# Rotary query and key rows: copied out of PSUM by ScalarE, multiplied in place by VectorE one slot later, subtracted in the next; other pairs of tiles, moved stores, a split first norm

## The chip, the core and the metric

The kernel runs on one core of one Trainium2 chip. The metric is the device time in microseconds of one execution. Each core has TensorE (PE, matrix products into the PSUM banks), VectorE (DVE), ScalarE (ACT), GpSimd (POOL) and SyncE (SP, which here only issues DMAs). Engines run their own instruction streams in order and meet through semaphores.

## The reference, cut to what matters

The input x is (2, 512, 512). Two blocks of the form x = x + s * silu(g) follow each other. In the first, s is attention and g a gated feed-forward network, both of the same normed rows:

```python
qkv = hidden_states @ qkv_w + qkv_b              # 512 -> 3 * 512, 32 heads of 16
q = _rope(q, cos, sin); k = _rope(k, cos, sin)   # [x1*cos - x2*sin, x2*cos + x1*sin]
scores = jnp.einsum('bqhd,bkhd->bhqk', q, k) * scale
probs = jax.nn.softmax(scores + (1.0 - causal) * MASK_VAL, axis=-1)
ctx = jnp.einsum('bhqk,bkhd->bqhd', probs, v).reshape(b, s, e)
return ctx @ out_w + out_b
# the feed-forward part: silu(xt @ W_gate.T) * (xt @ W_up.T) @ W_down.T, 1376 wide
```

In the second block s is a four-layer recurrent network (a scan with complex decay, then a small MLP, per layer) and g a feed-forward network with ternary weights in an octonion arrangement. Everything is float32; products that need the precision are split into a rounded high part and a low part and take three passes.

## The kernel before, in words

The two sequences b = 0, 1 go through block 0 one after the other, then both through block 1 together. In block 0 the weights come in **units** of 128 x 512. Unit u is loaded by SP into `raw`, rounded to `w_hi` by ACT or POOL, and `w_lo = raw - w_hi` is made by POOL. Units 0 and 1 are the first 128 columns of Q and K, units 2 to 5 are V, and `Q_UNIT`, `K_UNIT` and `FFN_UNIT` give the places of the rest. Each Q, K or feed-forward unit becomes one **job**: twelve matmuls of 128x512 (L942 to L944) into one of two banks `proj_ps`.

The attention part is a table of **slots**. In slot s (0 to 47) PE multiplies the scores of one pair of heads (L972, group of tiles x = s % 3), VectorE adds the mask and takes the row maxima (L1486, `row_maxima`), and PE may only start the scores of slot s + 1 when these are done (`part_ready`). Five slots behind (`LAG`) PE makes the transposed scores (L981, `scores_T`) and ACT their exponentials (L1344), which PE waits for before the next transposed scores (`probs_ready`). The rest of PE's slot is two "triples" of the running job (`fill`), the product with V, and turns. One sequence has 65 slots; in the last 17 come the down projection and the turns of the next norm. Every engine runs the same table: `for s in range(SLOTS)` with `units_after(s)` (the jobs that ended in slot s - 1), `rest_in_slot`, `written_in`, `read_in` and `raw_in_slot` saying what it does in slot s.

A Q or K job is followed by the rotation: three VectorE instructions that read the bank in PSUM, add the bias and multiply by the cosine or sine (`rope_first`, L1538 to L1542), in the slot in which the job is known to be done, behind that slot's row maxima. One slot later VectorE adds the two halves (`rope_second`, L1553), ACT rounds the sum (`rope_hi`, L1278), POOL makes the low part (`rope_lo`, L770), and SP writes all of it to DRAM (`write_rows`, L660 and L662). `read_rows` (L675) brings it back as the stacks `q_st` and `k_st` of one group of four heads; group g is needed by the scores of slot 6g.

SP's queue is in order. At slot 1 of the first sequence it also holds six stores of the ternary weights (L708), in front of the read of group 1. The first norm: VectorE takes statistics of four tiles (L1499), then aggregates (L1502), POOL makes the inverse deviation of all four at once (L833, L835), VectorE scales (L1508), PE turns 16 blocks (L1018), ACT and VectorE split them (L1262, L1475).

## Time and profile before

| | |
|---|---|
| median of 3 runs | 640.64 us (639.93, 640.64, 642.9) |
| the profiled execution's own time | 639.16 us |
| its span (first to last instruction) | 637.3 us |
| outside the span | 1.9 us |
| PE busy | 603.5 us, 95% |
| VectorE busy | 383.8 us, 60% |
| GpSimd busy | 376.9 us, 59% |
| ScalarE busy | 276.7 us, 43% |

Busy shares say which engine has no time to spare on the whole; here it is PE. What a change can save is then the time in which PE stood, or ran at a lower clock. The ends of matmuls are modelled in the profile, so a short stall shows as less idle time than it cost: the start of one slot's scores to the start of the next is the safer measure.

### The profile page before, as it was taken

Reading aid. Unit: us, or ns where it says so; the run is one execution under the profiler, and the core shown is the slowest. Engines: PE = TensorE matmul, PEld = TensorE weight load, DVE = VectorE, ACT = ScalarE, POOL = GpSimd, SP = SyncE. Lnnn points to the kernel's source line nnn. Section 1 sums busy time; section 2 is a strip of 40 time slices with the busy share of each in tenths; the row PEclk is TensorE's granted clock in tenths of the full one; section 3 lists DMA queues with packets and bytes.
Section 4 is the critical chain, followed back from the end, with each engine's and each line's share of the span. In section 5 each row is a group of like instructions: output and inputs, shape, how many; then the busy total and the mean of one; then the engine's idle time right before and its main releaser. Section 6 shows DMA issues by size and latency. Waiting matters only on the chain.

```text
span 637.3 us, 9817 instructions
## 1 busy us (share of the span) xinstructions
PE 603.5 (95%) x3348; PEld 417.2 (65%) x3348; DVE 383.8 (60%) x920; ACT 276.7 (43%) x440; POOL 376.9 (59%) x596
## 2 busy tenths in 40 slices
PE   2998998999999999888999999999999999999996
PEld 2865565666657888655656665677878676767664
DVE  4957867666524587696686664264986261525257
ACT  3524554655553533054555556444222344332432
POOL 4875756655434577767566544345888676641264
PEclk9998999999999999999999999999999999999999
DMA  9768764744441335658568644643440000000002
GB/s 291 220 227 282 214 200 129 230 118 103 96 129 54 95 92 165 194 179 262 139 165 261 187 113 123 259 161 115 144 164 1 0 1 1 1 1 0 1 30 103
DMA packets 60369, 83.63 MB, mean 131 GB/s; under 512 B 17936, under 2 KB 26768, under 8 KB 60320
## 3 DMA queue, kind: packets, MB, share of 16 engines
q1 hardware_dynamic: 57392, 73.70, 39.2%
q10 hardware_dynamic: 2928, 9.31, 4.0%
q8 instruction: 27, 0.44, 0.3%
q14 instruction: 22, 0.18, 0.1%
HBM read 65.17 MB, written 26.99 MB: 145 GB/s over the span
## 4 chain that ended last, share of the span: by engine, by line
PE 73%; DVE 9%; DMA 6%; POOL 4%; issue 3%; SPq 2%; ACT 2%; ACTq 0%; POOLq 0%; DVEq 0%
PE proj_ps L942 8%; PE ctx_ps L1097 6%; PE proj_ps L943 6%; PE proj_ps L944 6%; PE score_ps L972 5%; PE proj_ps L1145 3%; PE proj_ps L1146 3%; PE scoreT_ps L981 3%; DMA k_st<-rows 3%; PE score_ps L942 2%; PE score_ps L944 2%; PE score_ps L943 2%; PE ctx_ps L1145 2%; PE scoreT_ps L1145 2%; PE scoreT_ps L1146 2%
## 5 line engine op out<-in xcount | busy, mean ns | idle before, releaser
L761 POOL TENSOR_TENSOR w_lo<-raw,w_hi 128x512 fp32r<-128x512 f32 x98 | 133.1, 1363 | 68.1 <-ACT w_hi L1300 61.7
L1486 DVE CUSTOM_DVE_ANT_0 score_ps<-score_ps,causal 128x512 f32<-128x512 f32 (+3 forms) x256 | 119.9, 516 | 59.5 <-PE score_ps L972 59.0
L1344 ACT ACTIVATE probs_T<-scoreT_ps 128x1024 f32<-128x1024 f32 (+1 forms) x96 | 84.9, 884 | 79.1 <-PE scoreT_ps L981 78.6
L942 PE MATMUL proj_ps<-xn_hi,w_hi 128*128 128x512 f32 x224 | 99.9, 446 | 0.3 <-POOL w_lo L761 0.3
L943 PE MATMUL proj_ps<-xn_hi,w_lo 128*128 128x512 f32 x224 | 88.3, 394 | 0.0
L944 PE MATMUL proj_ps<-xn_lo,w_hi 128*128 128x512 f32 x224 | 88.2, 394 | 0.0
L759 POOL TENSOR_SCALAR w_hi<-raw 128x512 fp32r<-128x512 f32 x50 | 31.2, 625 | 49.7 <-PE proj_ps L944 47.2
L942 PEld LDWEIGHTS proj_ps<-xn_hi,w_hi 128*128 128x128 f32 x224 | 42.0, 187 | 24.6 <-issue 9.8
L972 PE MATMUL score_ps<-k_st,q_st 50*128 50x512 f32 (+3 forms) x256 | 44.7, 386 | 13.2 <-DVE row_max L1486 7.8
L972 PEld LDWEIGHTS score_ps<-k_st,q_st 50*128 50x128 f32 x256 | 21.8, 186 | 53.8 <-issue 26.8
L795 POOL TENSOR_SCALAR_AFFINE_SELECT probs_T<-probs_T 128x256 f32<-128x256 f32 x128 | 49.6, 410 | 9.8 <-ACT probs_T L1344 9.8
L917 POOL TENSOR_TENSOR hsL<-hidden_T,hsH 128x256 fp32r<-128x256 f32 x44 | 38.0, 882 | 26.6 <-ACT hsH L1427 26.1
L944 PEld LDWEIGHTS proj_ps<-xn_lo,w_hi 128*128 128x128 f32 x224 | 42.2, 188 | 9.8
L1097 PE MATMUL ctx_ps<-probs_T,V 128*32 128x128 f32 (+3 forms) x512 | 47.7, 445 | 0.0
L943 PEld LDWEIGHTS proj_ps<-xn_hi,w_lo 128*128 128x128 f32 x224 | 42.5, 190 | 5.0
L1269 ACT ACTIVATE q_st<-one_turn_ps 2x512 fp32r<-2x512 f32 x64 | 37.5, 585 | 18.8 <-PE one_turn_ps L958 18.5
L1616 DVE TENSOR_TENSOR hsl<-hidden_T,hsh 128x512 fp32r<-128x512 f32 x22 | 16.2, 735 | 40.9 <-ACT hsh L1367 40.9
L981 PE MATMUL scoreT_ps<-q_st,k_st 50*128 50x512 f32 (+3 forms) x256 | 37.5, 329 | 0.7 <-ACT probs_T L1344 0.7
L1300 ACT ACTIVATE w_hi<-raw 128x512 fp32r<-128x512 f32 x48 | 30.0, 625 | 18.1 <-PE one_turn_ps L944 6.9
L1486 DVE DVE_READ_ACCUMULATOR2_ANT row_max<- 128x1 f32 x256 | 35.5, 139 | 0.3
L925 POOL TENSOR_TENSOR inv_std<-var_eps,half 128x8 f32<-128x8 f32 x9 | 14.8, 1646 | 34.6 <-DVE var_eps L1760 34.6
L1278 ACT ACTIVATE rows_hi<-turned_rows 128x512 fp32r<-128x512 f32 x16 | 10.1, 632 | 49.8 <-DVE turned_rows L1553 41.6
(306 smaller groups left out, 1317.2 us busy)
## 6 DMA issues: line engine op xcount, KB each, us to landing
raw<-w SPq DMA_DIRECT2D x98, 256.0 KB, 2.8
rows<-rows_hi SPq DMA_DIRECT2D x32, 256.0 KB, 3.7
arranged<-tern SPq DMA_DIRECT2D x96, 85.0 KB
q_st<-rows SPq DMA_DIRECT2D x32, 200.0 KB
k_st<-rows SPq DMA_DIRECT2D x32, 200.0 KB
rows<-rows_lo SPq DMA_DIRECT2D x16, 256.0 KB, 4.5
gate_w<-arranged ACTq DMA_DIRECT2D x4, 704.0 KB, 7.1
up_w<-arranged ACTq DMA_DIRECT2D x4, 704.0 KB, 8.4
```

Of the source, the lines that this page charges most:

```text
L761: nc.gpsimd.tensor_tensor(w_lo[n % SPLIT][:, :], raw[n % RAW][:, :], F32(w_hi[n % SPLIT][:, :]), ALU.subtract).then_inc(unit_ready, 1)
L795: m = nc.gpsimd.affine_select(out=halves[:, :, c:c + P], in_=halves[:, :, c:c + P], pattern=[[0, 2], [1, P]], compare_op=ALU.is_ge, fill=0 ...
L917: nc.gpsimd.tensor_tensor(hsL[d % HS][:, :], hidden1_T[:, f, 256 * pr:256 * pr + 256], F32(hsH[d % HS][:, :]), sub).then_inc(hs1_ready, 1)
L942: nc.tensor.matmul(acc, lh, rh, start=first, stop=False)
L943: nc.tensor.matmul(acc, ll, rh, start=False, stop=False)
L944: return nc.tensor.matmul(acc, lh, rl, start=False, stop=last)
L972: m = nc.tensor.matmul(score_ps[:, hh, c:c + (qt + 1) * P], q[:, qt * P:(qt + 1) * P], k[:, 0:(qt + 1) * P], start=part == 0, stop=True, s ...
L981: m = nc.tensor.matmul(scoreT_ps[:, hh, c:c + S - kt * P], k[:, kt * P:(kt + 1) * P], q[:, kt * P:], start=part == 0, stop=True, skip_grou ...
L1097: m = nc.tensor.matmul(ctx_ps[32 * h:32 * h + 32, kt * P:S], V[:, kt, (4 * g + h) * 32:(4 * g + h + 1) * 32], probs_T[(gp + h // 2) % 4][: ...
L1145: nc.tensor.matmul(hid1_ps[u % 4], lhs, xh[:, kc, :], start=kc == 0, stop=False)
L1344: nc.scalar.activation(probs_T[gp % 4][:, c:c + 2 * w].rearrange("p (h c) -> p h c", h=2), scoreT_ps[:, :, 0:w], ACT.Exp, scale=0.25).then ...
L1486: m = nc.vector.tensor_tensor_reduce(out=block, in0=block, in1=causal[:, S - w:], scale=1.0, scalar=-3e38, op0=ALU.add, op1=ALU.max, accum ...
```

## The change

The diff, with small parts left out:

```diff
@@ -52,8 +52,8 @@
...
 UNITS = U_OUT + KC
-Q_UNIT, K_UNIT, V_UNIT = (0, 9, 12, 18), (1, 10, 13, 19), 2
-FFN_UNIT = [6, 7, 8, 11, 14, 15, 16, 17] + list(range(20, 34))
+Q_UNIT, K_UNIT, V_UNIT = (0, 8, 12, 18), (1, 9, 13, 19), 2
+FFN_UNIT = [6, 7, 10, 11, 14, 15, 16, 17] + list(range(20, 34))
 IN_FRONT = 3 * KC
...
 TRIPLES = (U_DOWN - FILL) * KC
@@ -62,6 +62,10 @@
 FFN_OF = {u: w for w, u in enumerate(FFN_UNIT)}
+COPIED = [u for u in sorted(QK_OF) if u >= FILL]
 def job(u):
...
@@ -103,15 +107,15 @@
 def rest_in_slot(s):
-    return [u for u in sorted(QK_OF) if u >= FILL and unit_slot(u) + 3 == s]
+    return [u for u in sorted(QK_OF) if u >= FILL and unit_slot(u) + 4 == s]
 def written_in(s):
-    return [u for u in sorted(QK_OF) if u >= FILL and unit_slot(u) + 4 == s]
+    return [u for u in sorted(QK_OF) if u >= FILL and unit_slot(u) + 5 == s]
 def read_in(s):
-    return next((g for g in range(1, GROUPS) if (1 if g == 1 else max(6 * g - 6, unit_slot(K_UNIT[g // 2]) + 6)) == s), None)
+    return next((g for g in range(1, GROUPS) if (1 if g == 1 else max(6 * g - 6, unit_slot(K_UNIT[g // 2]) + 7)) == s), None)
 def down_in(s):
@@ -191,6 +195,7 @@
 HI_BY_ACT = FILL + 3
...
 RAW, SPLIT = 4, 5
+WARM = 10
 COPIES = (50, 49)
...
@@ -631,7 +637,13 @@
...
-        return proj_free, JOBS * b + job(u) + 1
+        return job_released(b, job(u))
+    def job_released(b, n):
+        copied_jobs = [job(u) for u in COPIED]
+        if n in copied_jobs:
+            return rope_copied, len(COPIED) * b + copied_jobs.index(n) + 1
+        return proj_free, (JOBS - len(COPIED)) * b + sum(k not in copied_jobs for k in range(n + 1))
...
@@ -639,7 +651,7 @@
         def _(sp):
...
                 sp.dma_start(X[:, t, :], x_dram[0, t]).then_inc(x_in[t], 16)
-                if t == 0:
+                if t == NT - 1:
                     sp.dma_start(ident[:, :], A["ident"]).then_inc(ident_in, 16)
...
@@ -701,17 +713,16 @@
                         write_rows(b, K_UNIT[0])
...
                 for s in range(SCORE_SLOTS + 1):
-                    if b == 0 and s == 1:
-                        for w in range(3):
-                            sp.wait_ge(wp_ready, w + 1)
-                            for x, src in enumerate((tern_pos[w], tern_neg[w])):
-                                sp.dma_start(tern_d[w][x].rearrange("(p n) -> p n", p=P), F32(src[:, :])).then_inc(tern_stored, 16)
                     for u in written_in(s):
...
                         read_rows(b, read_in(s))
-                    for u in raw_in_slot(s):
+                    for x, u in enumerate(raw_in_slot(s)):
                         load(b, u)
+                        if b == 0 and s == 0 and 1 <= x <= 3:
+                            sp.wait_ge(wp_ready, x)
+                            for half, src in enumerate((tern_pos[x - 1], tern_neg[x - 1])):
+                                sp.dma_start(tern_d[x - 1][half].rearrange("(p n) -> p n", p=P), F32(src[:, :])).then_inc(tern_stored, 16)
                     if b == 0 and s == 3:
...
                     for x in range(copies_in(b, s)):
@@ -831,11 +842,16 @@
...
                 nc.gpsimd.tensor_scalar(var_eps0[:, :], mean_var[:, :, 1], EPS, 1.0, ALU.add, ALU.mult).then_inc(eps_added, 1)
-                pool.wait_ge(eps_added, k + 1)
+                pool.wait_ge(eps_added, k + 2)
                 nc.gpsimd.tensor_tensor(rstd[:, :], var_eps0[:, :], half[:, 0:NT], ALU.pow).then_inc(rstd_ready, 1)
             pool.wait_ge(ones_set, 2)
-            norm_rstd(0)
+            for x in range(2):
+                pair = slice(2 * x, 2 * x + 2)
+                pool.wait_ge(mv_ready, 2 * x + 2)
+                nc.gpsimd.tensor_scalar(var_eps0[:, pair], mean_var[:, pair, 1], EPS, 1.0, ALU.add, ALU.mult).then_inc(eps_added, 1)
+                pool.wait_ge(eps_added, x + 1)
+                nc.gpsimd.tensor_tensor(rstd[:, pair], var_eps0[:, pair], half[:, 0:2], ALU.pow).then_inc(rstd_ready, 1)
             for b in range(B):
...
                 for u in range(FILL):
@@ -982,8 +998,6 @@
                                              start=part == 0, stop=True, skip_group_check=part > 0)
...
-            pe.wait_ge(ident_in, 16)
             def norm_turn(k, chunks=range(KC)):
                 pe.wait_ge(xn_ready, NT * (k + 1))
@@ -999,7 +1013,7 @@
                 if kc == 0:
...
                     if job(u) >= 2:
-                        pe.wait_ge(proj_free, JOBS * b + job(u) - 1)
+                        pe.wait_ge(*job_released(b, job(u) - 2))
                     elif b:
...
                 wh, wl = unit(b, u)
@@ -1012,6 +1026,10 @@
                 for k in triples_in(s):
...
+            pe.wait_ge(ones_set, 2)
+            for n in range(WARM):
+                nc.tensor.matmul(proj_ps[1][:, 0:P], V[:, 0, 0:P], V[:, 0, 0:P], start=True, stop=True)
+            pe.wait_ge(ident_in, 16)
             for t in range(NT):
...
                 for kc in range(KC):
...
@@ -1276,6 +1294,16 @@
                 if r >= 2:
...
                 nc.scalar.activation(rows_hi[t][:, :], turned_rows[t][:, :], ACT.Copy).then_inc(rows_hi_ready, 1)
+            def rope_copy(b, u):
+                (t, c), r = QK_OF[u], rope_job(b, u)
+                ps, bias = job_bank(u), qk_bias[:, 4 * t + c:4 * t + c + 1]
+                act.wait_ge(proj_done, JOBS * b + job(u) + 1)
+                act.wait_ge(turned_ready, r - 1)
+                nc.scalar.activation(by_cos[t][:, :], ps[:, :], ACT.Identity, bias=bias)
+                nc.scalar.activation(by_sin[t][0:64, :], ps[64:128, :], ACT.Identity, bias=bias[64:128])
+                nc.scalar.activation(by_sin[t][64:128, :], ps[0:64, :], ACT.Identity, bias=bias[0:64]).then_inc(rope_copied, 1)
...
@@ -1352,7 +1380,9 @@
                     for u in units_after(s):
...
                             ffn_tanh(b, u)
-                    for u in units_after(s - 1):
+                        else:
+                            rope_copy(b, u)
+                    for u in units_after(s - 2):
                         if u in QK_OF:
...
                     if max_in(s) is not None:
@@ -1381,7 +1411,7 @@
                         act.wait_ge(arranged, 16 * len(ARRANGE))
...
                         load_rows(W_UP, up_w1, tu_in, range(2, KC))
-                    if b == B - 1 and s == LAST_DOWN - 1:
+                    if b == B - 1 and s == LAST_DOWN - 2:
...
                                          (bout[:, :], A["bout"].partition_broadcast(P))):
@@ -1494,16 +1524,28 @@
                 if k:
...
                 for t in range(NT):
-                    if k == 0:
-                        dve.wait_ge(x_in[t], 16)
                     nc.vector.bn_stats(stat[:, t, :], NORM[k][0][:, t, :]).then_inc(stats, 1)
...
+            def first_stats(t):
+                dve.wait_ge(x_in[t], 16)
+                nc.vector.bn_stats(stat[:, t, :], X[:, t, :]).then_inc(stats, 1)
+                dve.wait_ge(stats, t + 1)
+                nc.vector.bn_aggr(mean_var[:, t, :], stat[:, t, :]).then_inc(mv_ready, 1)
+            def first_rows(t):
+                dve.wait_ge(mv_ready, t + 1)
+                dve.wait_ge(rstd_ready, t // 2 + 1)
+                nc.vector.tensor_scalar(xn_first[:, t, :], X[:, t, :], mean_var[:, t, 0:1], rstd[:, t:t + 1],
+                                        ALU.subtract, ALU.mult).then_inc(xn_ready, 1)
             def norm_rows(k):
                 dve.wait_ge(mv_ready, NT * (k + 1))
-                dve.wait_ge(rstd_ready, k + 1)
+                dve.wait_ge(rstd_ready, k + 2)
                 for t in range(NT):
...
                                             ALU.subtract, ALU.mult).then_inc(xn_ready, 1)
@@ -1542,6 +1584,13 @@
                 nc.vector.scalar_tensor_tensor(out=by_sin[t][64:128, :], in0=ps[0:64, :], scalar=bias[0:64], in1=rope_sin[0:64, :],
...
+            def rope_times(b, u):
+                (t, c), r = QK_OF[u], rope_job(b, u)
+                dve.wait_ge(*released(b, u))
+                nc.vector.tensor_tensor(by_cos[t][:, :], by_cos[t][:, :], rope_cos[:, :], ALU.mult).then_inc(cos_ready, 1)
+                nc.vector.tensor_tensor(by_sin[t][:, :], by_sin[t][:, :], rope_sin[:, :], ALU.mult).then_inc(sin_half, 1)
             def rope_second(b, u):
                 (t, c), r = QK_OF[u], rope_job(b, u)
@@ -1550,7 +1599,9 @@
                 dve.wait_ge(*released(b, u))
...
                     dve.wait_ge(rows_lo_ready, r - 1)
-                nc.vector.tensor_tensor(turned_rows[t][:, :], by_cos[t][:, :], by_sin[t][:, :], ALU.add).then_inc(turned_ready, 1)
+                nc.vector.tensor_tensor(turned_rows[t][:, :], by_cos[t][:, :], by_sin[t][:, :], ALU.subtract if u in COPIED else ALU.add)\
+                    .then_inc(turned_ready, 1)
...
@@ -1558,8 +1609,10 @@
                     rope_first(b, u)
...
-            norm_stats(0)
-            norm_rows(0)
+            for t in range(NT):
+                first_stats(t)
+            for t in range(NT):
+                first_rows(t)
             norm_lo(0)
...
             nc.vector.tensor_copy(ident_r[:, :], ident[:, :]).then_inc(ident_rounded, 1)
@@ -1583,7 +1636,8 @@
                         nc.vector.scalar_tensor_tensor(out=tern_neg[w][:, :], in0=tern_w[w][:, :], scalar=theta[:, 1, w:w + 1], in1=tern_over[w][:, :],
...
                 for u in units_after(0):
-                    ffn_out(b, u)
+                    if u in FFN_OF:
+                        ffn_out(b, u)
                 for s in range(SLOTS):
...
                         row_maxima(b, s)
@@ -1602,14 +1656,15 @@
                                                 c3[:, :, 0:D].rearrange("p (t h) d -> p t h d", t=NT),
...
                                                 ALU.mult).then_inc(turn_done(n), 1)
+                    for u in units_after(s - 2):
+                        if u in QK_OF:
+                            rope_second(b, u)
                     for u in units_after(s - 1):
                         if u in QK_OF:
-                            rope_second(b, u)
+                            rope_times(b, u)
                     for u in units_after(s) if s else ():
...
                             ffn_out(b, u)
-                        else:
-                            rope_first(b, u)
                     if parted_in(s) is not None:
...
```

In words: in the slot in which a Q or K job (other than the first two) is known to be done, ACT copies the bank out, with the bias, in three ACTIVATEs (`rope_copy`); they free the bank, so PE now waits on `rope_copied` for it. VectorE multiplies both copies in place one slot later (`rope_times`, two instructions of 128x512), and subtracts them one slot after that. Six jobs per sequence go this way, twelve in all. One pair of tiles of Q and K moves to units 8 and 9 (from 9 and 10), so that its rows are written and read back a slot or more earlier; the later pairs are written a slot later. The ternary stores stand between the weight loads of slot 0. The first norm is split into two halves, ten matmuls on a tile of ones (`WARM`) precede the first turns, `ident` is loaded behind X, and four DMA issues on ACT's queue stand one slot earlier near the end of block 0.

VectorE's order around the job of unit 12, which ends in slot 7 of a sequence (`proj_ps` holds it; the rows are those of slots 8 to 10, the maxima rows that repeat left out). Before:

```order
L1486 ISA score_ps,row_max<-score_ps,causal 128x256
L1486 ISA row_max 128x1
L1538 SCALAR_TENSOR_TENSOR by_cos_79<-proj_ps,qk_bias,rope_cos 128x512
L1540 SCALAR_TENSOR_TENSOR by_sin_81<-proj_ps,qk_bias,rope_sin 64x512
L1542 SCALAR_TENSOR_TENSOR by_sin_81<-proj_ps,qk_bias,rope_sin 64x512
L1486 ISA score_ps,row_max<-score_ps,causal 128x512
L1486 ISA row_max 128x1
...
L1553 TENSOR_TENSOR turned_rows_83<-by_cos_79,by_sin_81 128x512
L1486 ISA score_ps,row_max<-score_ps,causal 128x384
```

Now:

```order
L1516 ISA score_ps,row_max<-score_ps,causal 128x256
L1516 ISA row_max 128x1
...
L1516 ISA score_ps,row_max<-score_ps,causal 128x512
L1516 ISA row_max 128x1
L1591 TENSOR_TENSOR by_cos_79<-by_cos_79,rope_cos 128x512
L1592 TENSOR_TENSOR by_sin_81<-by_sin_81,rope_sin 128x512
L1516 ISA score_ps,row_max<-score_ps,causal 128x384
L1516 ISA row_max 128x1
...
L1603 TENSOR_TENSOR turned_rows_83<-by_cos_79,by_sin_81 128x512
```

Three instructions between the maxima of slots 8 and 9 are gone; two stand between those of slots 9 and 10, and the subtraction is behind the maxima of slot 10.

ScalarE's order in the same slots (`probs_T` are the exponentials, `q_st` the rows of maxima). Before:

```order
L1344 ACTIVATE probs_T_95<-scoreT_ps 128x1024 x2
L1278 ACTIVATE rows_hi_85<-turned_rows_83 128x512
L1269 ACTIVATE q_st_90<-one_turn_ps 2x512 x2
L1344 ACTIVATE probs_T_95<-scoreT_ps 128x512
L1344 ACTIVATE probs_T_96<-scoreT_ps 128x1024 x2
```

Now:

```order
L1372 ACTIVATE probs_T_95<-scoreT_ps 128x1024
L1304 ACTIVATE by_cos_79<-proj_ps,qk_bias 128x512
L1305 ACTIVATE by_sin_81<-proj_ps,qk_bias 64x512
L1306 ACTIVATE by_sin_81<-proj_ps,qk_bias 64x512
L1372 ACTIVATE probs_T_95<-scoreT_ps 128x1024
L1287 ACTIVATE q_st_90<-one_turn_ps 2x512 x2
L1372 ACTIVATE probs_T_95<-scoreT_ps 128x512
L1296 ACTIVATE rows_hi_85<-turned_rows_83 128x512
L1372 ACTIVATE probs_T_96<-scoreT_ps 128x1024
```

Three copies have come between the exponentials of slots 8 and 9, and the rounding of the rows has moved from in front of the maxima rows to behind the next exponential.

SyncE's order at slots 0 and 1 of the first sequence. Before:

```order
L652 DMA raw_101<-w 128x512
L708 DMA tern<-tern_pos_151 128x680
L708 DMA tern<-tern_neg_154 128x680
L708 DMA tern<-tern_pos_152 128x680
L708 DMA tern<-tern_neg_155 128x680
L708 DMA tern<-tern_pos_153 128x680
L708 DMA tern<-tern_neg_156 128x680
L675 DMA q_st_90<-rows 50x2x512 x2
```

Now:

```order
L664 DMA raw_101<-w 128x512
L725 DMA tern<-tern_pos_151 128x680
L725 DMA tern<-tern_neg_154 128x680
L664 DMA raw_102<-w 128x512
L725 DMA tern<-tern_pos_152 128x680
L725 DMA tern<-tern_neg_155 128x680
L664 DMA raw_103<-w 128x512
L725 DMA tern<-tern_pos_153 128x680
L725 DMA tern<-tern_neg_156 128x680
L664 DMA raw_100<-w 128x512
L664 DMA raw_101<-w 128x512
L687 DMA q_st_90<-rows 50x2x512 x2
```

The read of group 1 (`q_st_90`) has no store right in front of it any more.

## Rows read from the trace of the kernel before

**Rows 1.** The page, busy time of TensorE.

```profile
PE 603.5 (95%) x3348; PEld 417.2 (65%) x3348; DVE 383.8 (60%) x920; ACT 276.7 (43%) x440; POOL 376.9 (59%) x596
```

**Rows 2.** Timeline, PE, score matmuls: start, us, instruction, count [idle before <-releaser].

```profile
269.84 0.44 PE L972 MATMUL score_ps<-k_st,q_st 50*128 50x384 f32 x2 [0.66 <-DVE row_max L1486]
272.07 0.39 PE L972 MATMUL score_ps<-k_st,q_st 50*128 50x256 f32 x2
275.18 0.50 PE L972 MATMUL score_ps<-k_st,q_st 50*128 50x512 f32 x2 [0.90 <-DVE row_max L1486]
277.67 0.50 PE L972 MATMUL score_ps<-k_st,q_st 50*128 50x384 f32 x4
...
281.34 0.50 PE L972 MATMUL score_ps<-k_st,q_st 50*128 50x512 f32 x2
284.81 0.45 PE L972 MATMUL score_ps<-k_st,q_st 50*128 50x384 f32 x2 [0.77 <-DVE row_max L1486]
287.05 0.38 PE L972 MATMUL score_ps<-k_st,q_st 50*128 50x256 f32 x2
291.37 0.50 PE L972 MATMUL score_ps<-k_st,q_st 50*128 50x512 f32 x2 [1.48 <-DMA k_st<-rows]
...
329.48 0.44 PE L972 MATMUL score_ps<-k_st,q_st 50*128 50x384 f32 x2 [0.92 <-DVE row_max L1486]
```

**Rows 3.** Timeline, VectorE, slots 8 and 9 of the second sequence.

```profile
281.07 0.75 DVE L1538 SCALAR_TENSOR_TENSOR by_cos<-proj_ps,qk_bias,rope_cos 128x512 f32<-128x512 f32 x1
```

**Rows 4.** Line queries: duration ns min/median/max of one.

```profile
L1553 DVE TENSOR_TENSOR turned_rows<-by_cos,by_sin x16: 685/694/1076, 20.5 to 329.3; 128x512 f32<-128x512 f32 x16
L761 POOL TENSOR_TENSOR w_lo<-raw,w_hi x98: 1265/1293/1920, 11.8 to 440.3; 128x512 fp32r<-128x512 f32 x98
```

**Rows 5.** Groups of ACT by form: count | busy us, mean ns | idle before.

```profile
L1393 ACT ACTIVATE ctx_hi<-proj_ps,v_bias 128x512 fp32r<-128x512 f32 x4 | 2.7, 683 | 0.0
```

**Rows 6.** The view of waits, PE, whole span: us in total, times, longest.

```profile
PE scoreT_ps L981 <- ACT probs_T L1344: 0.7, 2, 0.4
```

**Rows 7.** Timeline, ScalarE, slots 9 and 10 of the second sequence.

```profile
282.25 1.03 ACT L1344 ACTIVATE probs_T<-scoreT_ps 128x1024 f32<-128x1024 f32 x1 [0.60 <-PE scoreT_ps L981]
285.34 0.63 ACT L1278 ACTIVATE rows_hi<-turned_rows 128x512 fp32r<-128x512 f32 x1 [2.06 <-DVE turned_rows L1553]
```

**Rows 8.** Timeline, TensorE, first sequence, in slot 11.

```profile
70.58 0.50 PE L981 MATMUL scoreT_ps<-q_st,k_st 50*128 50x512 f32 x2 [0.38 <-ACT probs_T L1344]
```

**Rows 9.** Timeline, first sequence, start of slot 1, on PE.

```profile
42.73 0.44 PE L972 MATMUL score_ps<-k_st,q_st 50*128 50x384 f32 x2 [0.76 <-DVE row_max L1486]
```

**Rows 10.** Timeline, SP's queue and PE, first sequence, slots 1 to 6.

```profile
46.77 1.20 SPq L708 DMA_DIRECT2D tern<-tern_neg  x1
48.02 1.83 SPq L675 DMA_DIRECT2D q_st<-rows  x2
...
56.51 0.50 PE L972 MATMUL score_ps<-k_st,q_st 50*128 50x512 f32 x2 [2.19 <-DMA k_st<-rows]
```

**Rows 11.** Windows: us, busy PE PEld DVE ACT POOL (x), PEclk, DMA share, GB/s.

```profile
57.90:61.30 3.40, 3.40 (x16) 2.50 (x15) 1.73 (x6) 1.74 (x4) 2.36 (x5) 0.51 0.82 289
```

**Rows 12.** Timeline, the head: VectorE, TensorE, ScalarE.

```profile
9.79 1.92 DVE L1508 TENSOR_SCALAR xn_first<-X,mean_var,rstd 128x512 f32<-128x512 f32 x4 [1.59 <-POOL rstd L835]
...
10.48 0.45 PE L1018 MATMUL one_turn_ps<-ident,xn_first 128*128 128x128 f32 x1 [10.48 <-DVE xn_first L1508]
...
13.07 0.42 PE L1018 MATMUL one_turn_ps<-ident,xn_first 128*128 128x128 f32 x1
...
14.90 0.50 PE L942 MATMUL score_ps<-xn_hi,w_hi 128*128 128x512 f32 x1 [0.98 <-DVE xn_lo L1475]
```

**Rows 13.** Timeline, ScalarE, the first sum of absolute weights.

```profile
16.74 0.76 ACT L1289 ACTIVATE tern_over<-tern_w 128x680 f32<-128x680 f32 x1
```

**Rows 14.** The page of DMA issues, SP: out<-in, count, KB, median us to landing.

```profile
tern_w<-tern_w SPq DMA_DIRECT2D x3, 340.0 KB, 6.0
```

**Rows 15.** Timeline, TensorE, end of block 0's second sequence.

```profile
439.98 0.66 PE L938 MATMUL one_turn_ps<-ident,ctx_rows 128*128 128x128 f32 x4 [1.14 <-DVE ctx_lo L1626]
```

5 lines of the change are left out of this document (3 added, 2 removed).

## The prediction

> **What bounds the kernel now.** I read the page's busy times first: TensorE is busy for 603.5 us of a span of 637.3 [rows 1], so only what lets it stand, or slows it, can be won. Then the timeline of TensorE's score matmuls, by the start of each slot [rows 2]. A slot that has score group x = 0 and the turns of the maxima lasts 2.49 us where nothing holds it (275.18 to 277.67), and 3.47 where a rotation lies behind its maxima (281.34 to 284.81): 0.98 lost. The reader should see the pattern behind it: idle times of 0.66, 0.90, 0.77 and 0.92 us, all ended by VectorE's row maxima, stand at the places where VectorE was still at the rotation. The fifth such place in this sequence is before slot 23. By the view of waits TensorE waited for the exponentials only twice, 0.7 us together [rows 6]: ScalarE, 43% busy, has been out of its way.
>
> The profiled execution took 639.16 us, 1.48 less than the median of 640.64. I sum against 639.16 and shift the result to the median.
>
> **Rotation, each sequence.** Before, three VectorE instructions of 0.75 us each [rows 3], 2.25 in all, follow a slot's maxima, and TensorE's next slot waits for maxima queued behind them. Five of six jobs cost: slots 3, 5, 9, 22 and 24. Slots 5 and 24 have 0.90 and 0.92 idle, slot 9 loses 0.98 by its starts and slot 3 has 0.66 idle of which some 0.5 is net of a later slot (3.00 against 2.49 long); slot 22 is like it with 0.7. I take 0.5 + 1.0 + 1.0 + 0.7 + 1.0 = 4.2 a sequence, 8.4 in all; the idle entries alone, 0.66 + 0.90 + 0.77 + 0.7 + 0.92 = 3.95, would make 7.9. The job of unit 13 costs nothing visible now.
>
> After, VectorE has two multiplications, 1.4 us by the subtraction's 0.69 [rows 4], one slot after the copies, and the subtraction, 0.69, one slot later. A lone 0.69 behind the maxima costs nothing today (slots 4, 10). 1.4 is 0.85 less than 2.25, so where 2.25 lost 1.0 it loses 0.15, except where the multiplications fall on a slot whose maxima already set its length. With 2.23-us slots of x = 1 of that kind (269.84 to 272.07 [rows 2]) I estimate 0.3 at slot 2, 0.1 at slot 4 and 0.4 at slot 10: 0.8 a sequence, 1.6 in all. Bounds: 0, if all of it lies beside other work, and 1.4 x 12 = 16.8 if none does.
>
> ScalarE takes on three copies. The nearest row is its reading of a PSUM bank with a bias, 0.68 for 128x512 [rows 5]; reading SBUF it is 0.63, and an exponential twice as wide takes 1.03, so 0.52 a half [rows 7]. Three copies are 1.6 to 2.05 us, I take 1.9, twelve times 23 us of ScalarE's idle time. They free the bank, which before was freed by VectorE at 2.25 after its maxima; the job after next wants it at least a slot and a half later, so this costs nothing. The rounding of the rows moves two slots on: where it stood ahead of the exponentials it held ScalarE for 2.06 us, waiting for VectorE's sum [rows 7]. That wait goes, as the sum is by then long done. The copy itself waits for its job's last matmul, which ended in the slot before.
>
> Net of this part: 8.4 - 1.6 = **6.8 us**.
>
> **Pair 8, 9 instead of 9, 10.** Stack g2 is needed at slot 12. In the second sequence slot 11 (287.05 to 291.37, 4.32 long) ends in a wait for its DMA, 1.48 idle [rows 2]. Slot 5 of the same group lasts 3.11 with a rotation's 0.98, so 2.13 is clean and slot 11 loses 2.19. The units come a slot earlier for Q and for K, and the read is issued at slot 8 instead of 9, a slot being worth 2.2 to 2.5 us: it just covers the 2.19. In the first sequence TensorE waits there for the exponentials, 0.38 idle [rows 8], as ScalarE has been held by the same rounding; I count 0.65 by the slot's length. Sum **2.8 us**, bounds 0.6 (the transfer is as late as before) and 2.8.
>
> **Ternary stores.** At slot 1 of the first sequence the read of group 1 is issued at 48.02, right behind the last store [rows 10], while slot 1 begins at 42.73 [rows 9]: 5.3 us, of which some 0.8 are SP's own issues. Slot 6 then stands 2.19 us for this transfer [rows 10]. Of the 2.19, 0.98 would be the rotation's, as in the second sequence, and is counted above; 1.3 is this wait's (the slot is 2.28 longer than clean). With the read 4.5 us earlier it goes. The stores stand between weight loads one slot earlier; they delay the loads of three units, which have a slot or more of slack. 
>
> **Slot 0, first sequence.** The product of unit 8 stood behind the first maxima there; slot 1 starts with 0.76 idle [rows 9]. Unit 8 is now a K or Q tile and VectorE has nothing at slot 0: **0.8 us**, bounds 0 and 0.8. ScalarE's three copies stand there instead, ahead of no exponential.
>
> **Head.** The inverse deviations of all four tiles come 1.59 us after the statistics; the four scalings take 1.92 from 9.79, the 16 turns start at 10.48 and are 0.216 apart (12 of them to 13.07), and the first projection starts at 14.90 [rows 12]. Split by halves, the first two tiles are scaled while the second half's deviation is made; the last is ready about 10.6 instead of 11.7, and only its four turns remain. With ten matmuls ahead, the turns should be as fast as at the other end of the kernel, four in 0.66 [rows 15]. The last turn ends at about 11.3 and the first projection, 1.38 behind ScalarE's first rounding now (13.52), starts at about 12.4: 2.5 us earlier. But the products with V behind the two projections need the sums of absolute weights. The first now starts at 16.74 and takes 0.76 [rows 13]; their DMA lands some 6.0 us after its issue [rows 14], about 16.2, so the third sum is done at 16.2 + 3 x 0.78 = 18.6, and V starts at 18.7 instead of 20.6. I take **1.9 us**; bounds 0.5 (the weights' load moves on too) and 2.65 (nothing else is late).
>
> The Trainium skill ("TensorE: Matmul & The Clock Gate", Part 1: The HAM clock gate) says that an idle TensorE goes to the lower level and that earlier matmuls lift it. By that rule the ten matmuls pay and the stop ahead of slot 6 costs twice, and rows 11 agree for the stop (after 2.19 us of standing [rows 10]); for the head only the 0.216 between turns speaks for the lower level. Without the rule's part the head would be 0.5 us later at the turns, and V's start would not move.
>
> **Tail.** At the end of block 0's second sequence TensorE stands 1.14 us for `ctx_lo` [rows 15], behind ScalarE's DMA issues. One slot earlier they are out of the way of ScalarE's context rounding, but stand in front of other work: **0.15 us**, bounds -0.3 and 1.14.
>
> **Port contention.** The multiplications read two SBUF tiles; `rope_first` read one and PSUM. The subtraction, of the same kind, has a median of 694 ns but takes 1076 at worst, and GpSimd's `w_lo` 1293 and 1920 [rows 4]. I take **-0.8 us**, bounds 0 and -5.
>
> The Trainium skill ("SBUF — State Buffer", SBUF: two separate sides) says that a VectorE operation with two SBUF inputs and a GpSimd operation that reads SBUF hold a shared port pair exclusively, each for the whole instruction. The longest of rows 4 agree, 0.38 and 0.63 above the median, their medians do not; by that rule in full, each of 24 multiplications could wait 1.29. This speaks against the change, and is rival 2 below, priced from rows.
>
> **Sum.** 6.8 + 2.8 + 2.8 + 0.8 + 1.9 + 0.15 - 0.8 = 14.45, say 14.5. 639.16 - 14.5 = 624.7; to the median + 1.48: **626.1**, forecast 626.0.
>
> **Rivals.**
> 1. The row transfers stay late. They are written one slot later for every pair but the first and read only then; if the DMA, not the issue, is the limit, the 2.19 of slot 11 and the 1.3 of slot 6 stay in good part. For it: 1.48 idle on the transfer alone; against: the clear 5.3 us of queue. It gives back 3.3: 629.4.
> 2. Port contention at the worst of each kind: 24 multiplications at 1.076 instead of 0.69 are 9.2 us, of which about half shows behind maxima: 4.2 more than taken, 630.3. Against it is the median.
> 3. ScalarE takes VectorE's place in part. In the slot of the copies it has 2 x 1.03 + 1.9 = 3.96 us of work in a slot of 2.23 to 2.49. If TensorE waits 0.3 us of it per job, 12 x 0.3 = 3.6: 629.7. For it: rows 8; against: rows 6.
> 4. The other side: the same, without any slack behind. The exponentials of the copies' slot come 3.96 - 2.23 = 1.73 us late and TensorE waits for all of it at 12 jobs, 20.8 us, in place of the 1.6 taken above as new cost: 14.45 + 1.6 - 20.8 = -4.75, so 639.16 + 4.75 + 1.48 = 645.4. It decides where the wait exceeds some 1.3 us a job (16 / 12). Against it: the next slots have 2.06 + 0.63 of work at most, and the transposed scores run five slots behind.
>
> **How the numbers follow.** Chances: the forecast 0.58, rival 1 0.17, rival 2 0.10, rival 3 0.10, rival 4 0.05. The forecast's own range, from the bounds of the head, the tail and the slots, is 623 to 629. Rivals 1 to 3 end at 629.4 to 630.3, two together at 633; 622.5 to 632.5 leaves out rival 4, most of such pairs and a tail of the forecast. 0.5% of 640.6 is 3.2 us, about what can be told from no change: faster means below 637.4, slower above 643.8. All cases but rival 4 and a mixture halfway to it are faster: 0.94, 0.03 and 0.03.
>
> **What would show it.** Right: score slots 3, 5, 9, 22 and 24 without idle time ended by the maxima; at 57 to 61 us no granted clock of 0.5; slot 11 of the second sequence about 2.1 long; the read of group 1 issued within a microsecond of slot 1; V's first product about 18.7; ScalarE's waits for `turned_rows` gone; TensorE's waits for exponentials under 2 us in all. Wrong: idle entries of the score matmuls ended by `k_st` (rival 1), multiplications of `rope_times` with a median near 1.0 us (rival 2), transposed scores that wait for `probs_T` in the slots after a copy (rivals 3 and 4), or a V stage that starts where it does now, at 20.6. If the sum is right but the time is not, the loss should lie in the 17 slots after the scores or in block 1, which this sum leaves alone.

## The result, and the profile after

The changed kernel takes 634.1 us (median of 6 runs, 631.3 to 636.1); the kernel before 641.05 (median of 6, 637.7 to 642.9). The ratio is 0.9891, with a 95% interval of 0.9865 to 0.9916: 7 us faster, where 14.5 were forecast and 626.0 was the time. The direction was right; the time lies 1.6 us above the range's upper end (632.5).

The profiled execution took 631.3 us, 7.9 below the 639.16 of before. The page's busy times, to be read against [rows 1]:

```profile
PE 605.8 (96%) x3368; PEld 419.6 (67%) x3368; DVE 382.3 (61%) x908; ACT 300.0 (48%) x476; POOL 384.5 (61%) x598
```

ScalarE has taken on 23.3 us, as priced (23). VectorE has given up only 1.5 us, though 36 instructions of 0.75 us became 24 that were priced at 0.69: 10.4 us should have gone. That is the first sign of what failed.

TensorE's score matmuls in the second sequence, slots 4 to 13 (columns as in [rows 2]), with one row that stands inside slot 12:

```profile
264.44 0.50 PE L988 MATMUL score_ps<-k_st,q_st 50*128 50x384 f32 x4
268.20 0.39 PE L988 MATMUL score_ps<-k_st,q_st 50*128 50x256 f32 x2 [1.68 <-DVE row_max L1516]
270.34 0.50 PE L988 MATMUL score_ps<-k_st,q_st 50*128 50x512 f32 x2
272.83 0.50 PE L988 MATMUL score_ps<-k_st,q_st 50*128 50x384 f32 x4
275.06 0.39 PE L988 MATMUL score_ps<-k_st,q_st 50*128 50x256 f32 x2
276.50 0.50 PE L988 MATMUL score_ps<-k_st,q_st 50*128 50x512 f32 x2
279.09 0.50 PE L988 MATMUL score_ps<-k_st,q_st 50*128 50x384 f32 x4
...
281.78 0.39 PE L988 MATMUL score_ps<-k_st,q_st 50*128 50x256 f32 x2
283.92 0.51 PE L988 MATMUL score_ps<-k_st,q_st 50*128 50x512 f32 x2
286.17 0.47 PE L958 MATMUL proj_ps<-xn_hi,w_hi 128*128 128x512 f32 x1 [0.62 <-ACT by_sin L1306]
288.26 0.51 PE L988 MATMUL score_ps<-k_st,q_st 50*128 50x384 f32 x4
```

The stalls of [rows 2] are gone: slot 5 lasts 2.14, slot 9 2.59, and slot 11 2.14 with no DMA behind it. But slot 4 lasts 3.76 instead of 2.23, and slot 12 4.34 instead of 3.49. The idle column shows only 0.62 of slot 12's 0.85; the starts are the measure.

Lengths of the slots that moved, by the starts of their score matmuls in the profiled executions (us; first / second sequence; clean is what the slot takes where nothing holds it; for slot 3 the prediction's 2.49 stands, though it takes 2.26):

| slot | before | clean | after |
|---|---|---|---|
| 0 | 2.85 / 2.02 | 2.02 | 2.03 / 2.01 |
| 2 | 1.88 / 1.90 | 1.88 | 2.50 / 2.45 |
| 3 | 3.02 / 3.00 | 2.49 | 2.26 / 2.27 |
| 4 | 2.23 / 2.23 | 2.23 | 3.77 / 3.77 |
| 5, 6, 7 | 10.58 / 7.84 | 6.86 | 6.86 / 6.86 |
| 9 | 3.47 / 3.47 | 2.49 | 2.57 / 2.59 |
| 10 | 2.24 / 2.24 | 2.24 | 2.66 / 2.69 |
| 11 | 2.78 / 4.32 | 2.13 | 2.14 / 2.14 |
| 12 | 3.48 / 3.49 | 3.48 | 4.34 / 4.34 |
| 22, 23, 24 | 10.00 / 9.98 | 8.30 | 8.84 / 8.86 |
| 26 | 2.02 / 2.02 | 2.02 | 2.18 / 2.18 |

So the rotation's stalls fell from 8.4 us not to 1.6 but to 8.0: 0.6 at slot 2, 1.5 at slot 4, 0.1 at 9, 0.4 at 10, 0.9 at 12, 0.5 at 23 and 0.2 at 26, less 0.2 at slot 3, 4.0 a sequence. (With 2.26 as the clean length of slot 3 both sums would be 0.5 larger, and their difference the same.) Between the last scores of the first sequence and the first of the second lie 91.6 us instead of 90.8.

VectorE across slots 3 and 4, and GpSimd beside it:

```profile
264.19 1.40 DVE L1591 TENSOR_TENSOR by_cos<-by_cos,rope_cos 128x512 f32<-128x512 f32 x1
265.51 1.09 DVE L1592 TENSOR_TENSOR by_sin<-by_sin,rope_sin 128x512 f32<-128x512 f32 x1
...
268.01 0.68 DVE L1603 TENSOR_TENSOR turned_rows<-by_cos,by_sin 128x512 f32<-128x512 f32 x1
```

```profile
263.75 1.29 POOL L781 TENSOR_TENSOR rows_lo<-turned_rows,rows_hi 128x512 fp32r<-128x512 f32 x1 [0.39 <-ACT rows_hi L1296]
265.00 1.07 POOL L770 TENSOR_SCALAR w_hi<-raw 128x512 fp32r<-128x512 f32 x1
266.15 1.57 POOL L772 TENSOR_TENSOR w_lo<-raw,w_hi 128x512 fp32r<-128x512 f32 x1
```

The first multiplication begins while `rows_lo` runs (to 265.04) and ends 0.55 later; the second ends 0.53 behind the end of `w_hi` (266.07). Each ends about half a microsecond after GpSimd's instruction ends, as if it had waited for that. GpSimd's instructions behind them are longer too: `w_hi` takes 1.07 instead of 0.62, `w_lo` 1.57 instead of 1.29.

Over the whole execution, from the queries of the two lines (min/median/max in ns):

```profile
L1591 DVE TENSOR_TENSOR by_cos<-by_cos,rope_cos x12: 686/985/1401, 42.2 to 320.8; 128x512 f32<-128x512 f32 x12
L1592 DVE TENSOR_TENSOR by_sin<-by_sin,rope_sin x12: 683/1096/1765, 43.0 to 322.2; 128x512 f32<-128x512 f32 x12
```

The same query for the instruction of the kernel before that reads PSUM and one SBUF tile:

```profile
L1538 DVE SCALAR_TENSOR_TENSOR by_cos<-proj_ps,qk_bias,rope_cos x12: 741/747/748, 46.1 to 325.7; 128x512 f32<-128x512 f32 x12
```

It never varied, though `w_lo` or `rows_lo` ran beside most of them. ScalarE ahead of slot 12:

```profile
282.51 0.63 ACT L1296 ACTIVATE rows_hi<-turned_rows 128x512 fp32r<-128x512 f32 x1 [0.99 <-DVE turned_rows L1603]
283.05 1.01 ACT L1372 ACTIVATE probs_T<-scoreT_ps 128x1024 f32<-128x1024 f32 x1
283.96 0.68 ACT L1304 ACTIVATE by_cos<-proj_ps,qk_bias 128x512 f32<-128x512 f32 x1
284.65 0.69 ACT L1305 ACTIVATE by_sin<-proj_ps,qk_bias 64x512 f32<-64x512 f32 x1
285.35 0.68 ACT L1306 ACTIVATE by_sin<-proj_ps,qk_bias 64x512 f32<-64x512 f32 x1
286.05 1.03 ACT L1372 ACTIVATE probs_T<-scoreT_ps 128x1024 f32<-128x1024 f32 x1
```

Its rounding of the rows still waits for VectorE's sum (24.6 us in all, against 41.6 before), and the three copies end at 286.03, where TensorE wanted the bank at 285.5.

In slot 10 it is not the bank. There the exponentials start right behind the copies, and TensorE waits for them before its transposed scores:

```profile
278.09 0.68 ACT L1306 ACTIVATE by_sin<-proj_ps,qk_bias 64x512 f32<-64x512 f32 x1
278.80 1.02 ACT L1372 ACTIVATE probs_T<-scoreT_ps 128x1024 f32<-128x1024 f32 x1
```

```profile
279.88 0.39 PE L997 MATMUL scoreT_ps<-q_st,k_st 50*128 50x256 f32 x2 [0.29 <-ACT probs_T L1372]
315.78 0.50 PE L997 MATMUL scoreT_ps<-q_st,k_st 50*128 50x512 f32 x2 [0.28 <-ACT probs_T L1372]
```

The second of these rows is in slot 23. With the two of the first sequence that makes four such waits, 1.1 us by the idle column. By the starts, the transposed scores of slot 10 come 0.79 us behind its scores, against 0.34 in slot 7, which has the same work: these 0.45 us are all that slot 10 lost.

The head and the first read of rows, TensorE, ScalarE and SP's queue:

```profile
9.54 0.27 PE L1036 MATMUL proj_ps<-ident,xn_first 128*128 128x128 f32 x1
9.65 0.27 PE L1036 MATMUL scoreT_ps<-ident,xn_first 128*128 128x128 f32 x1
...
12.04 0.50 PE L958 MATMUL score_ps<-xn_hi,w_hi 128*128 128x512 f32 x1 [1.08 <-DVE xn_lo L1505]
18.55 0.35 PE L1049 MATMUL proj_ps<-abs_sums,V 128*128 128x3 f32 x2 [0.74 <-ACT tern_over L1317]
```

```profile
16.03 0.77 ACT L1317 ACTIVATE tern_over<-tern_w 128x680 f32<-128x680 f32 x1 [2.07 <-DMA tern_w<-tern_w]
```

```profile
42.95 0.76 SPq L687 DMA_DIRECT2D q_st<-rows  x2
```

The turns are 0.11 apart, not 0.216 [rows 12]; the first projection starts 2.9 us earlier, and V's stage waits for the sums, as forecast. The read is issued at 42.95 instead of 48.02 [rows 10]. At the end of block 0's second sequence TensorE waits longer than in [rows 15]:

```profile
432.75 0.66 PE L954 MATMUL one_turn_ps<-ident,ctx_rows 128*128 128x128 f32 x4 [1.47 <-DVE ctx_lo L1681]
```

### The profile page after: what moved, and what is told of

Its sections match the earlier page's. It is cut to its first block, busy times and chain, and to the rows that moved or that the text cites. A ratio compares the mean times of both kernels' runs of the same rounds, so it can differ in the third digit from the quotient of the medians.

```text
span 629.4 us, 9886 instructions
## 1 busy us (share of the span) xinstructions
PE 605.8 (96%) x3368; PEld 419.6 (67%) x3368; DVE 382.3 (61%) x908; ACT 300.0 (48%) x476; POOL 384.5 (61%) x598
## 4 chain that ended last, share of the span: by engine, by line
PE 50%; ACT 2%; DVE 2%; POOL 2%; issue 1%; ACTq 0%; POOLq 0%; DVEq 0%
PE proj_ps L958 4%; PE proj_ps L1163 3%; PE proj_ps L1164 3%; PE ctx_ps L1115 3%; PE proj_ps L959 3%; PE proj_ps L960 3%; PE score_ps L988 2%; PE ctx_ps L1163 2%; PE scoreT_ps L1163 2%; PE ctx_ps L1164 2%; PE scoreT_ps L1164 2%; PE scoreT_ps L997 2%; PE one_turn_ps L1242 1%; POOL hsL L933 1%; PE proj_ps L1170 1%; PE score_ps L1262 1%
## 5 line engine op out<-in xcount | busy, mean ns | idle before, releaser
L770 POOL TENSOR_SCALAR w_hi<-raw 128x512 fp32r<-128x512 f32 x50 | 34.1, 681 | 41.7 <-PE proj_ps L960 37.3
L806 POOL TENSOR_SCALAR_AFFINE_SELECT probs_T<-probs_T 128x256 f32<-128x256 f32 x128 | 52.3, 428 | 11.4 <-ACT probs_T L1372 11.4
L1397 ACT ACTIVATE hsh<-hidden_T 128x512 fp32r<-128x512 f32 x22 | 13.9, 631 | 39.2 <-PE score_ps L960 39.2
```

What stands on the lines that cost most here:

```text
L806: m = nc.gpsimd.affine_select(out=halves[:, :, c:c + P], in_=halves[:, :, c:c + P], pattern=[[0, 2], [1, P]], compare_op=ALU.is_ge, fill=0 ...
```

## The experiments

Two theories stood after this reading. **P**: multiplications with two SBUF inputs wait for GpSimd's instructions that read SBUF. **S**: ScalarE gets to the copies late and is long at them, so TensorE waits for the bank that they free, or for the exponentials behind them. The rival to both was the prediction's own step, that the copies pay 6.8 us. Ratios are against the kernel before, with 95% intervals; the changed kernel's is 0.9891.

**e1, the rotation given back to VectorE.**

```diff
-COPIED = [u for u in sorted(QK_OF) if u >= FILL]
+COPIED = []
...
-                    for u in units_after(s - 1):
+                    for u in units_after(s):
                         if u in QK_OF:
-                            rope_times(b, u)
...
+                            rope_first(b, u)
...
```

With it the sum, the rounding and the writing and reading of the rows go back one slot.

> The changed kernel with the rotation given back to VectorE (three instructions from PSUM behind the maxima of the slot in which the job is done, the sum one slot later, rows written and read at the old distances); head, moved stores, pair 8 and 9 and the tail stay as changed. Theory P (the multiplications in place lose to GpSimd's port what they save, and TensorE waits for ScalarE's copies): the twelve rotations then cost as much either way, and this kernel takes the changed kernel's time within 1.5 us, about 633 to 636; its slots 3, 5, 9, 22, 24 lose 0.5 to 1.0 us each again, and slots 4 and 12 lose nothing. The prediction's term (6.8 us for the copies): it is 6 to 7 us slower than the changed kernel, 640 to 642.

637.8 us, 0.9955 (0.9932 to 0.9978): 4 us slower than the changed kernel by the ratios, between the two expectations. Its stalls were 1.5 at slot 1 (the job of unit 8 now ends ahead of slot 0), 1.0 at 9, 0.65 at 11 (TensorE waits for the exponentials there, as in [rows 8]), 0.7 at 22 and 1.0 at 24, with the rest at slots 2 to 5. So the copies are worth 4 us beside the new pair, though only 0.4 against the stalls of the old placing: the new pair puts a rotation in front of a slot that VectorE fills, and without the copies that costs. Part of what this trace lost is the clock's: in the second sequence the granted clock fell to 0.68 and 0.75 (264 to 270) behind the stop of slot 1, and again to 0.68 (440 to 444) behind a wait of 2.04 us for `ctx_lo` at the end of block 0.

**e2, the low part of the weights filled with zeros.**

```diff
-                nc.gpsimd.tensor_tensor(w_lo[n % SPLIT][:, :], raw[n % RAW][:, :], F32(w_hi[n % SPLIT][:, :]),
-                                        ALU.subtract).then_inc(unit_ready, 1)
+                nc.gpsimd.memset(F32(w_lo[n % SPLIT][:, :]), 0.0).then_inc(unit_ready, 1)
```

> The changed kernel in which GpSimd fills w_lo with zeros instead of subtracting (the low part of the weights is left out of the products): the instruction reads nothing of SBUF. Theory P: multiplications that lay beside w_lo fall from 0.9 to 1.8 us towards 0.69, their mean under 0.85; those beside w_hi or rows_lo, which still read, stay long; slots 2, 4 and 23 lose 1 us less together in each sequence, and the time falls by 2 to 4 us. Rival (VectorE's long instructions are long for another reason, such as the copies' writing into the same rows): the mean stays near 1.0 us and the time within 1 us.

628.3 us, 0.9818 (0.9783 to 0.9853). Unit 13's multiplications fell from 1.12 and 1.76 us to 0.79 and 0.68, but those beside `w_hi` stayed at 1.10, and those beside `rows_lo` at 1.27 to 1.40. (The 1.12 and the 0.79 both lay beside `w_hi` and ended 0.54 behind it; that one only began later. The 1.76 was `w_lo`'s.) The mean of all 24 went from 1.06 to 0.92 us, where under 0.85 was expected. Slot 4 fell by 0.3, slot 2 by 0.1, slots 12 and 23 not at all. 2.3 us of the gain came from the stretch between the sequences, which GpSimd's shorter work shortens: the time was no clean test, the durations were.

**e5, GpSimd fills `w_hi` and `rows_lo` as well.** The edit of `w_lo` is that of e2.

```diff
-                    nc.gpsimd.tensor_scalar(w_hi[n % SPLIT][:, :], raw[n % RAW][:, :], 1.0, 0.0, ALU.mult, ALU.add).then_inc(hi_done, 1)
+                    nc.gpsimd.memset(F32(w_hi[n % SPLIT][:, :]), 0.0).then_inc(hi_done, 1)
...
-                nc.gpsimd.tensor_tensor(rows_lo[t][:, :], turned_rows[t][:, :], F32(rows_hi[t][:, :]), ALU.subtract).then_inc(rows_lo_ready, 1)
+                nc.gpsimd.memset(F32(rows_lo[t][:, :]), 0.0).then_inc(rows_lo_ready, 1)
```

> The changed kernel in which GpSimd fills w_lo, its share of w_hi, and rows_lo with zeros (those parts of the weights and of the rotated rows are left out of the products): of GpSimd's long instructions none reads SBUF. Theory P: every multiplication and subtraction of VectorE that lay beside them falls to 0.68 to 0.70 us, and slot 4 loses 0.3 to 0.6 us against 2.24 instead of 1.54, slot 2 0.3 instead of 0.55; slots 10, 12 and 23 stay as long as they are, since they wait for ScalarE. Rival (slot 4 is long by VectorE's own work): slot 4 stays above 3.4 us.

625.1 us, 0.9765 (0.9715 to 0.9815). The two lines of the multiplications, and slot 4 of the second sequence:

```profile
L1590 DVE TENSOR_TENSOR by_cos<-by_cos,rope_cos x12: 686/690/693, 42.4 to 314.9; 128x512 f32<-128x512 f32 x12
L1591 DVE TENSOR_TENSOR by_sin<-by_sin,rope_sin x12: 682/684/894, 43.0 to 315.5; 128x512 f32<-128x512 f32 x12
```

```profile
260.09 0.50 PE L987 MATMUL score_ps<-k_st,q_st 50*128 50x384 f32 x4
262.51 0.39 PE L987 MATMUL score_ps<-k_st,q_st 50*128 50x256 f32 x2 [0.33 <-DVE row_max L1515]
```

Slot 4 lasts 2.42 and slot 2 1.93; slots 10 and 23 stay, 12 falls only to 4.08. P is shown: it held 0.5 us at slot 2 and 1.35 at slot 4 of each sequence, and the 0.2 of slot 26 (2.01 now). It is the same two instructions, in the same place; only what GpSimd did beside them differs. The two long ones left (0.894 each) lay beside the causal mask, an in-place instruction of GpSimd. As with e2 the time is no clean test: 2.3 us of it came from the stretch between the sequences, and slot 5 of the first sequence rose to 2.80, because TensorE, earlier now, waits 0.60 us for the stack of group 1.

**e3, two copies instead of three.**

```diff
-                nc.scalar.activation(by_sin[t][0:64, :], ps[64:128, :], ACT.Identity, bias=bias[64:128])
-                nc.scalar.activation(by_sin[t][64:128, :], ps[0:64, :], ACT.Identity, bias=bias[0:64]).then_inc(rope_copied, 1)
+                nc.scalar.activation(by_sin[t][:, :], ps[:, :], ACT.Identity, bias=bias).then_inc(rope_copied, 1)
```

> The changed kernel with two copies of 128x512 on ScalarE instead of three (by_sin is copied in one instruction, so its halves are not exchanged and the rotation is wrong by that). Theory S (TensorE waits for its bank because ScalarE gets to the copies late and they take 3 x 0.69): slot 12 loses 0.2 instead of 0.85 us in each sequence, slots 2 and 4 stay as they are, time 1.0 to 1.8 us below the changed kernel. If only the ports matter, slot 12 stays at 4.34 us and the time within 0.5 us.

628.6 us, 0.9828 (0.9793 to 0.9863): 4 us below the changed kernel by the ratios. Its slots 9 to 12 of the second sequence:

```profile
276.84 0.50 PE L988 MATMUL score_ps<-k_st,q_st 50*128 50x384 f32 x4
279.07 0.39 PE L988 MATMUL score_ps<-k_st,q_st 50*128 50x256 f32 x2
281.22 0.50 PE L988 MATMUL score_ps<-k_st,q_st 50*128 50x512 f32 x2
284.71 0.50 PE L988 MATMUL score_ps<-k_st,q_st 50*128 50x384 f32 x4
```

Slot 10 lasts 2.23 (2.37 in the first sequence) and slot 12 3.49; slot 23 is 2.57 again, and no wait for the exponentials is left. One instruction of 0.69 us held some 0.4, 0.9 and 0.5 us of each sequence, more than I had expected of it. Slot 4 stayed at 3.79. S is shown. P and S meet in slot 12 alone, which fell by 0.27 in e5: there the sum ahead of the rounding is free of `w_hi` (0.69 instead of 0.97), and rounding and copies come as much earlier.

**e4, the rounding one slot later on ScalarE.**

```diff
-                    for u in units_after(s - 2):
+                    for u in units_after(s - 3):
                         if u in QK_OF:
                             rope_hi(b, u)
```

> The changed kernel with the rounding of the rotated rows one slot later in ScalarE's order, behind that slot's exponentials and copies. Theory S: what makes the copies of unit 13 late is the rounding of unit 12 ahead of them, which waits 1 us for VectorE; with it gone TensorE's wait inside slot 12 (0.62 us idle, 0.85 by the slot's length) goes in both sequences, 1.7 us. Against it stands the second stack read, which goes out about a microsecond later; it has about 2 us of slack, so nothing is lost at slot 12. Rival (the copies are late by their own length): slot 12 stays at 4.2 us or more and nothing is gained.

641.9 us, 1.0021 (0.9994 to 1.0048): the whole gain gone, where 1.7 us were expected. The copies did start earlier in slot 11, but slot 12 grew to 6.3 us in the second sequence and 7.4 in the first, where the granted clock fell to 0.50 (72 to 75) behind the stop. GpSimd in slot 12 of the second sequence, and TensorE:

```profile
290.69 1.29 POOL L781 TENSOR_TENSOR rows_lo<-turned_rows,rows_hi 128x512 fp32r<-128x512 f32 x1 [2.60 <-ACT rows_hi L1296]
291.94 0.86 POOL L806 TENSOR_SCALAR_AFFINE_SELECT probs_T<-probs_T 128x256 f32<-128x256 f32 x1
```

```profile
293.32 0.43 PE L974 MATMUL one_turn_ps<-ident_r,max_cols 128*34 128x128 f32 x4 [2.30 <-POOL max_cols L795]
```

GpSimd's `rows_lo` kept its place and waited 2.60 us for the rounding, and behind it in the queue stood the maxima that TensorE turns. I had followed the moved instruction to the DMA it feeds, and not to the engine between.

**e6, one copy, the exchange on VectorE.**

```diff
...
+                nc.vector.tensor_tensor(by_sin[t][0:64, :], by_cos[t][64:128, :], rope_sin[64:128, :], ALU.mult).then_inc(sin_low, 1)
+                nc.vector.tensor_tensor(by_sin[t][64:128, :], by_cos[t][0:64, :], rope_sin[0:64, :], ALU.mult).then_inc(sin_half, 1)
...
```

ScalarE keeps the copy into `by_cos` alone; the product with the cosine stands one slot later, ahead of an addition.

> The changed kernel with one copy of 128x512 on ScalarE instead of three; VectorE makes the exchanged halves itself (two multiplications of 64x512 a slot later, then in the next slot the product with the cosine and an addition, four instructions instead of three). Theory S: slots 10, 12 and 23 fall to 2.24, 3.48 and 2.58 us, 1.85 a sequence. Against it, VectorE has one more instruction of 0.7 us, now two behind the maxima of slots 4 and 10: up to 0.6 us a slot there, and more where GpSimd reads beside it. Time 629 to 633, a gain of 1 to 4 us on the changed kernel. Rival (VectorE's share is what counts): no gain, slots 5 and 11 each lose what slots 10 and 12 win.

640.0 us, 0.9997 (0.9970 to 1.0025): a miss. With one more instruction that waits for GpSimd (up to 1.72 us), TensorE waited for the maxima 18 times, 13.2 us in all, against 5 times and 4.5 us in the changed kernel: slots 11, 25 and 26 lost 1.0, 0.65 and 0.95. VectorE was the tighter of the two engines.

**e7, the moved stores alone, on the kernel before.** The edit is that of the change, the stores between the loads of slot 0.

> The kernel before with one part of the change: the six stores of ternary weights between the loads of slot 0. The prediction's term: slot 5 of the first sequence falls from 4.41 to 3.1 us, slots 6 and 7 from 3.33 and 2.84 to 2.49 and 2.24 with no granted clock of 0.5 there, together 2.8 us; the time is 2 to 3.5 us below the kernel before. Rival (another transfer holds the stack read): slot 5 stays above 4 us and nothing is gained.

639.4 us, 0.9986 (0.9953 to 1.0018). In the trace slots 5, 6 and 7 of the first sequence took 3.11, 2.47 and 2.24 instead of 4.41, 3.33 and 2.84, 2.76 us less, as forecast, with a granted clock of 1.00 there. But the time did not follow. In that execution TensorE ran its first nine projections 0.43 us apart instead of 0.23 (slot 0 began 1.3 us later), slot 11 of the first sequence waited for its stack (4.42 instead of 2.78), and the stretch between the sequences was 1.0 longer, while slot 11 of the second was 1.0 shorter. A term can be right in its place and not be seen in the sum.

**e8, the tail's DMA issues put back.**

```diff
-                    if b == B - 1 and s == LAST_DOWN - 2:
+                    if b == B - 1 and s == LAST_DOWN - 1:
```

> The changed kernel with ScalarE's four DMA issues at the end of block 0 back in their old slot. If the one-slot move is what made TensorE's wait for ctx_lo longer there (1.47 against 1.14 us), the wait is 1.1 to 1.2 us again and the time 0.3 us lower, which only the trace can show. If it is not, the wait stays near 1.5 us.

633.5 us, 0.9888 (0.9832 to 0.9943), the same as the changed kernel. The wait for `ctx_lo` was 1.21 us, as expected. But in traces with the issues moved it was 0.58 (e10), 1.01 (e4) and 1.39 to 2.04 us (the rest), so this one trace does not show that the move costs 0.3. This trace showed something else, in both sequences, behind the stop of slot 4 (windows, columns as in [rows 11]):

```profile
270.50:273.60 3.10, 3.10 (x10) 1.90 (x10) 1.86 (x6) 1.54 (x2) 1.67 (x3) 0.64 0.73 218
273.60:276.60 3.00, 3.00 (x17) 2.22 (x16) 1.95 (x5) 1.03 (x1) 2.63 (x5) 0.81 0.65 216
```

Slots 5 and 6 took 3.16 and 2.98 instead of 2.13 and 2.49: 1.5 us lost a sequence, after 1.67 us in which TensorE stood.

**e10, no matmuls ahead of the turns.** The edit is `WARM = 0`.

> The changed kernel without the ten matmuls ahead of the first turns. If they are what makes the turns 0.11 us apart instead of 0.21, the turns are 0.21 apart again, and the first projection starts 0.3 to 1 us later; V's stage waits for the sums of absolute weights anyway and starts within 0.4 us of 18.8, unless the first projections run at the lower level too, which would cost up to 2 us there. Rival: turns and projections stay as they are.

632.5 us, 0.9905 (0.9873 to 0.9937), which cannot be told from the changed kernel; the trace can. The turns were 0.21 apart, and TensorE's first projections ran at half pace:

```profile
8.18 0.42 PE L1036 MATMUL proj_ps<-ident,xn_first 128*128 128x128 f32 x1
...
12.36 0.79 PE L958 MATMUL score_ps<-xn_hi,w_hi 128*128 128x512 f32 x1 [0.77 <-DVE xn_lo L1505]
13.81 0.63 PE L958 MATMUL score_ps<-xn_hi,w_hi 128*128 128x512 f32 x1
15.09 0.63 PE L958 MATMUL score_ps<-xn_hi,w_hi 128*128 128x512 f32 x1
16.31 0.40 PE L958 MATMUL score_ps<-xn_hi,w_hi 128*128 128x512 f32 x1
```

Three matmuls lie between two of these rows: 0.43 us each until 16.3, 0.23 after it. In e8, where the granted clock reads 0.50 for 53 to 56, they were 0.43 apart as well: that is the lower level, 1.2 GHz, and then the upper. The product of the sums ahead of V's stage started at 19.7 instead of 18.55; in the eleven traces of kernels with the ten matmuls it started at 18.25 to 19.11. Slot 0 began at 39.1, 0.9 us later than in the changed kernel's first trace, but with the ten matmuls it began anywhere from 37.7 to 39.2.

**e11, the changed kernel once more**, in one execution.

> The changed kernel once more, for its clock. The theory: the stop of 1.5 us in slot 4 is sometimes followed by a fall of the granted clock, which the profiled execution of 631.3 us does not show, and the time of such an execution is 1.5 us longer for each sequence in which it happens. Expected: slots 5 and 6 are either 2.14 and 2.49 us, at a granted clock of 1, or some 3.2 and 3.0 with a clock of 0.6 to 0.8, and nothing between; all other slots as in the first profile.

632.35 us. Slots 5 and 6 took 2.14 and 2.49 in both sequences, the clock at 1: the first of the two cases. The other was seen in e8, and in e10's second sequence in another form (slot 1 at 3.37 instead of 2.24, with a granted clock of 0.67 for 260 to 263). That such falls make up the distance of 2.8 us between the profiled 631.3 and the median of 634.1 fits, and the granted clock of the six runs goes the same way, 0.998 as the mean of the one of 631.3 us and 0.991 of the one of 636.1; only the profiled one has a trace, so it is not shown.

**e9, the cosine's product first, from PSUM.**

```diff
-                act.wait_ge(proj_done, JOBS * b + job(u) + 1)
+                act.wait_ge(cos_ready, r + 1)
...
-                nc.scalar.activation(by_cos[t][:, :], ps[:, :], ACT.Identity, bias=bias)
...
+                nc.vector.scalar_tensor_tensor(out=by_cos[t][:, :], in0=ps[:, :], scalar=bias, in1=rope_cos[:, :],
+                                               op0=ALU.add, op1=ALU.mult).then_inc(cos_ready, 1)
...
```

> The changed kernel with the rotation shared otherwise: VectorE makes the product with the cosine straight from the PSUM bank (one SBUF input) behind the maxima of the slot in which the copies stand now; ScalarE waits for it and copies only the two exchanged halves, which free the bank; VectorE multiplies those with the sine one slot later and adds up in the next, as now. Theories P and S together: the instruction from PSUM takes 0.75 us whatever GpSimd does, ScalarE has 1.38 us instead of 2.07; slots 10, 12 and 23 lose nothing, slots 2 and 4 less than 0.5 us each; 3 us a sequence, so the profiled execution is 6 us and more below the changed kernel's 631.3, 623 to 627. Rival (ScalarE's wait for VectorE makes the copies late again): slot 12 stays above 4 us and the gain is under 3 us.

630.7 us, 0.9872 (0.9849 to 0.9894), where 623 to 627 were expected. The product took 739 to 748 ns at all 12 jobs, and slots 2, 4, 10 and 12 fell to 1.91, 2.38, 2.3 and 3.79. But slots 3, 23 and 25 rose to 3.15, 3.33 and 4.32, the last as ScalarE waited 2.98 us for VectorE and then held the exponentials that TensorE wants.

**e12, each pair in the form that was shorter for it.**

```diff
+COS_FIRST = [u for u in COPIED if u < 18]
...
```

> A try for a better kernel out of two that were measured: the jobs of units 8, 9, 12 and 13 as in the kernel with the cosine's product first (its slots 2, 3, 4, 10 and 12 lost 1.5 us a sequence, the changed kernel's 3.3), those of units 18 and 19 with three copies as in the changed kernel (0.7 us against 2.1). Expected from these rows: slots 23, 25 and 26 as in the changed kernel (3.13, 2.97, 2.18), the others as in the other, 1.5 to 2 us a sequence below the changed kernel, so 627 to 629 in the profiled execution and 3 to 4 us by the ratio. Rival (the losses move instead of adding up): within 1 us of the kernel with the cosine's product first.

628.1 us, 0.9809 (0.9774 to 0.9843), with nothing left out: 5 us below the changed kernel by the ratios and 3.9 by the profiled executions, where 3 to 4 were expected. Its slots 4, 12 and 25 took 2.37, 3.78 and 2.96. It is the fastest complete kernel of this study, and it came from reading slot by slot which form lost less.

## Why the prediction was wrong

**The stalls that it saw went.** Slots 3, 5, 9, 22 and 24 are free of the maxima's wait, 8.4 us, as said.

**The step that failed** is the rotation's new cost: "1.4 is 0.85 less than 2.25, so where 2.25 lost 1.0 it loses 0.15", and from it "0.8 a sequence, 1.6 in all", with 0.8 more for the ports. It measured 8.0 against these 2.4. Two things are in it. The multiplications took 1.3 to 2.8 us a pair and not 1.4: 1.85 us a sequence at slots 2 and 4 (e5). And "They free the bank [...] so this costs nothing" did not hold: in slot 12 TensorE wanted the bank 0.6 us before ScalarE was through, and in slots 10 and 23 it waited for exponentials that the copies had put off, though "ScalarE's idle time" was to take them: 1.8 a sequence at the three slots (e3). Together 7.3 us of the 8.0. "That wait goes, as the sum is by then long done" was wrong as well: rounding and sum stand in the same slot of the two engines' tables, and ScalarE still waits 24.6 us.

**The rivals** 2 and 3 both came true: rival 2's 24 multiplications, priced at 1.076, cost 3.7 us of stall (the rival's price was 4.2 more than the 0.8 taken, though half of its 9.2 less 0.8 is 3.8), and rival 3's 3.6 us is what e3 gave back, half of it through the exponentials, as the rival had it (slots 10 and 23), and half through the bank (slot 12). The prediction's own signs of both were there: a median of the multiplications near 1.0 us (0.985 and 1.096), and transposed scores that wait for `probs_T` behind a copy. I had listed them as alternatives with a chance each and let the range end at one and a half of them. They have different causes, so nothing kept them from coming together: 626.1 + 4.2 + 3.6 = 633.9. That this meets the measured 634.1 is luck. In the profiled executions the sum missed by 6.6 us (624.7 against 631.3), of which 5.6 is the rotation's, and the median lies 2.8 above the profiled execution instead of the 1.48 that was added.

The Trainium skill ("SBUF — State Buffer", SBUF: two separate sides) says that the shared pair of ports is locked for a whole instruction and that the other engine blocks. I weighed it by medians of [rows 4], and most of those subtractions began while GpSimd stood or was nearly through: a median over mixed neighbours says nothing of a lock. By e5, and by the rows at 264.19 and 265.51, the rule holds here, for the two-input instruction against any of `w_lo`, `rows_lo` and `w_hi`, and against none of the fills. The rows of the kernel before had it: the subtraction of 1076 ns ended 0.54 behind a `w_hi`, the price of one neighbour, and the multiplications were to be placed where GpSimd has one at five of the six jobs of a sequence.

**Pair 8, 9** gave 2.82 us (2.8): slot 11 fell by 0.64 and 2.18. The agreement is partly luck, as slot 11 of the old placing lasted 4.42 and 3.30 in e7 where it had lasted 2.78 and 4.32. **The stores** gave 2.74 (2.8) in slots 5 to 7, the clock's part included. **Slot 0** gave 0.82 (0.8). **The head** gave 1.7 (1.9): the first projection came even earlier than said, at 12.04, and V's stage at 18.8 (18.7), bound by the load of the ternary weights. The prediction gave the ten matmuls a part in the turns alone. Without them nine projections ran at the lower level in e10, and in e7, but none in the kernel before, whose turns are 0.21 apart and whose projections are 0.23 apart nearly from the first; with them none did in eleven traces. The Trainium skill's rule of the clock ("TensorE: Matmul & The Clock Gate", Part 1: The HAM clock gate), that earlier matmuls lift it, agrees with e10 and e7; what it was worth in the time is not shown, as slot 0 of e10 began within the spread of the others.

**The tail** lost 0.33 in these two traces (0.15 gained was said; the bound was -0.3); by the spread given at e8 that is not shown to be the move's. And **the stretch between the sequences** lost 0.8, which was in no term: the first scores of the second sequence wait 1.74 instead of 0.99 us for their stack, and start 8.7 us after its read is issued instead of 7.6. In all other traces it was 8.2 to 9.5, also in e7 (8.5), which has only the stores moved. Why is open: the three loads of weights issued right behind it were on their way in the kernel before too, and that kernel has one trace only. Some 0.6 us came back in block 1.

The sum, then, in the profiled executions: 8.4 - 8.0 + 2.82 + 2.74 + 0.82 + 1.7 - 0.33 - 0.8 + 0.6 = 7.95, against 7.9 measured.

## What to carry to other kernels

Before moving work off PSUM into SBUF on VectorE, look at what GpSimd does in that very place: in these traces an instruction with a PSUM operand had one price, and one with two SBUF operands waited for the end of its neighbour on top of its own. When an instruction is moved in a table that all engines share, follow each of its readers in turn, with what is queued behind it, and not only the last. An engine that is 43% busy can still be late in one slot: the copies fitted into ScalarE's idle time on the whole, and not in slots 10, 12 and 23. And rivals with different causes add up: the range has to reach to their sum.

## What was not expected of the hardware

- VectorE's two-input instruction of 128x512 takes 0.68 to 0.69 us alone and up to 1.77 us beside GpSimd, ending some 0.5 us behind the GpSimd instruction that reads SBUF; GpSimd's fills (0.52 us) left it at 0.68. With one operand in PSUM (the product with the cosine) it took 735 to 752 ns in all fourteen traces.
- ScalarE's copy of 64 partitions of 512 takes as long as that of 128:

```profile
L1304 ACT ACTIVATE by_cos<-proj_ps,qk_bias x12: 676/681/689, 38.1 to 317.3; 128x512 f32<-128x512 f32 x12
L1305 ACT ACTIVATE by_sin<-proj_ps,qk_bias x12: 683/685/687, 38.8 to 318.0; 64x512 f32<-64x512 f32 x12
```

- Until 16.3 us in e10 the matmuls stood 0.43 us apart, as at the lower level in e8, and so ran at half their later pace while the granted clock read 1.00 for 12.3 to 16.3: at the head the column does not show the lower level, the distance of the matmuls does.
- A stop of 1.7 us of TensorE was followed by a granted clock of 0.64 and 0.81 in e8, and by none in the changed kernel's two traces, with the same instructions on either side.
